# The norm of x for QKV's last four blocks: on GpSimd instead of ScalarE, with loads, stores, moments, turns and parts at other steps

## The reference, cut to what matters

```python
def _layernorm(x, axis=-1, eps=1e-05):
    m = jnp.mean(x, axis=axis, keepdims=True)
    v = jnp.var(x, axis=axis, keepdims=True)
    return (x - m) / jnp.sqrt(v + eps)

# x: (2, 2048, 1024); attention with d = 256, one head
qkv = jnp.einsum('bsc,cf->bsf', _layernorm(x), Wqkv) + bqkv
q, k, v = split(qkv)
x = x + softmax(q @ k.T / 16) @ v @ Wo + bo
# FFN: relu(x @ up)^2 @ down, plus a routed low rank part, and a last layer norm
x = x + _L0_ffn_ref(_layernorm(x), ...)
```

## Time and profile before

| | us |
|---|---|
| median of three runs | 2342.77 (2338.67 to 2347.44) |
| the profiled execution's own time | 2346.55 |
| its span in the trace | 2344.7 |
| PE busy | 2306.0 (98% of the span) |
| VectorE, ScalarE, GpSimd busy | 1584.1, 825.3, 343.5 |
| mean granted TensorE clock | 0.993 of full |
| DMA, whole execution | 581.19 MB, mean 248 GB/s |

### The profile page before, as it was taken

How to read it: one execution, slowest core, us unless ns; L and a number is a source line. 1 busy time by engine, 2 the same in 40 slices (tenths; PEclk the granted TensorE clock), 3 DMA queues, 4 the chain that set the end, 5 groups by cost and what they waited for, 6 DMA issues and landing times.

```text
span 2344.7 us, 27515 instructions
## 1 busy us (share of the span) xinstructions
PE 2306.0 (98%) x10760; PEld 1934.2 (82%) x10760; DVE 1584.1 (68%) x1788; ACT 825.3 (35%) x949; POOL 343.5 (15%) x686
## 2 busy tenths in 40 slices
PE   9989899999999999999999999999999999999998
PEld 8878788888888888888888888888888888888886
DVE  6867658887898956498764368875238876434548
ACT  4335555666555533431212232213132121223211
POOL 2134500000131300032210013310003221000000
PEclk9999999999999999999999999999999999999999
DMA  9899874542233699978997678898668899666875
GB/s 295 291 363 301 305 247 138 209 142 82 96 116 114 232 302 334 329 260 304 346 325 215 190 251 295 324 331 279 190 223 270 306 326 337 208 194 201 244 206 194
DMA packets 242322, 581.19 MB, mean 248 GB/s; under 512 B 27345, under 2 KB 91793, under 8 KB 241937
## 3 DMA queue, kind: packets, MB, share of 16 engines
q1 hardware_dynamic: 160272, 443.56, 58.7%
q10 hardware_dynamic: 81280, 135.55, 15.8%
q0 software_dynamic: 640, 0.33, 0.1%
HBM read 422.25 MB, written 152.90 MB: 245 GB/s over the span
## 4 chain that ended last, share of the span: by engine, by line
PE 83%; DVE 6%; DMA 5%; ACT 2%; POOL 1%; issue 1%; SPq 1%; ACTq 0%; DVEq 0%; POOLq 0%
PE psum L1146 11%; PE psum L1147 11%; PE psum L1148 11%; PE psum L1125 10%; PE psum L1127 10%; PE psum L1126 10%; PE psum L1028 2%; PE psum L1029 2%; PE psum L1030 2%; PE psum L998 2%; PE psum L999 2%; PE psum L1000 2%; DMA RAW<-in_x_dram 1%; PE psum L1088 1%; PE psum L1081 1%
## 5 line engine op out<-in xcount | busy, mean ns | idle before, releaser
L1814 DVE TENSOR_TENSOR HB<-HB,psum 128x1024 f32<-128x1024 f32 x135 | 163.1, 1218 | 298.4 <-PE psum L1127 298.4
L2036 POOL TENSOR_SCALAR veA<-mvA 128x1 f32<-128x1 f32 x32 | 31.3, 977 | 1253.7 <-DVE mvA L1722 1253.7
L1381 ACT ACTIVATE HB<-HB 128x1024 f32<-128x1024 f32 x64 | 67.8, 1060 | 306.9 <-DVE HB L1814 306.9
L1125 PE MATMUL psum<-XS2h,WR 128*128 128x512 f32 x280 | 109.4, 391 | 1.0 <-DVE XS2l L1497 0.6
L1125 PE MATMUL psum<-XS1h,WR 128*128 128x512 f32 x280 | 109.1, 390 | 0.0
L1125 PE MATMUL psum<-XS0h,WR 128*128 128x512 f32 x280 | 109.1, 390 | 0.0
L1125 PE MATMUL psum<-XS3h,WR 128*128 128x512 f32 x280 | 109.1, 390 | 0.0
L1127 PE MATMUL psum<-XS1h,WR 128*128 128x512 f32 x280 | 109.0, 389 | 0.0
L1126 PE MATMUL psum<-XS2l,WR 128*128 128x512 f32 x280 | 109.0, 389 | 0.0
L1127 PE MATMUL psum<-XS2h,WR 128*128 128x512 f32 x280 | 109.0, 389 | 0.0
L1127 PE MATMUL psum<-XS0h,WR 128*128 128x512 f32 x280 | 109.0, 389 | 0.0
(11 more groups left out here) (439 smaller groups left out, 6706.7 us busy)
## 6 DMA issues: line engine op xcount, KB each, us to landing
WR<-wu_s SPq DMA_DIRECT2D x280, 512.0 KB, 4.4
WR<-wd_s SPq DMA_DIRECT2D x280, 512.0 KB, 4.9
att_s<-ATT ACTq DMA_DIRECT2D x32, 516.0 KB, 3.6
RAW<-in_x_dram SPq DMA_DIRECT2D x32, 512.0 KB, 9.4
RES<-x1b_s SPq DMA_DIRECT2D x128, 128.0 KB, 6.0
out_dram<-ZR ACTq DMA_DIRECT2D x118, 128.0 KB, 5.6
xT_s<-XT SPq DMA_DIRECT2D x24, 512.0 KB, 7.5
HB<-xT_s SPq DMA_DIRECT2D x12, 1024.0 KB, 8.8
```

What stands on the lines that cost most here:

```text
L1125: e.matmul(o, w[:, 0, ws], h[:, :, ws], start=kt == 0, stop=False)
L1814: e.tensor_tensor(to, a, src, op=ALU.add).then_inc(*vevac.next(key))
```

## The change

It takes `x_norm` off ScalarE's program. GpSimd does the same 16 operations (tensor_scalar, 128x256, x times RX plus NBX, in place) inside `x_merge`, right behind NBX and ahead of the copies of the moments. `x_turn` waits for GpSimd's signal. Beside it, steps stand at other places:

- the PE turns of x2 at g = 15, 16, 18, 19 (before 13 to 16), those of x3 at 25, 26, 28, 29 (before 25, 27, 29, 31);
- the loads of x5, x6, x7 one or two steps earlier and ahead of what else stands there (`front`), so on SP's queue they come ahead of the loads of quads u5, u7 and u9, where they stood behind these;
- the moments of x4 to x7 in two steps of two, at other steps;
- the turns of x4 to x7 four or five steps later, in the block ahead of their use, and the parts in pairs right behind, up to the first steps of the V tiles (for x4: in the last V tile and in the block's own first step);
- the last store of each of the quads u0 to u9 and d0 one step later.

```diff
-        at(g0, quad, q, [g0 + g for g in ((3, 4, 5, 5, 6, 7) if g0 < 37 else (4, 5, 6, 6, 7, 8))])
+        at(g0, quad, q, [g0 + g for g in ((3, 4, 5, 5, 6, 8) if g0 < 37 else (4, 5, 6, 6, 7, 9))])
...
-    for u, load, moments, norm, turns in ((2, 4, (9, 9, 9, 9), (11, 11, 12, 12), (13, 14, 15, 16)),
-                                          (3, 13, (17, 17, 18, 18), (20, 20, 21, 21), (25, 27, 29, 31))):
+    for u, load, moments, norm, turns in ((2, 4, (9, 9, 9, 9), (11, 11, 12, 12), (15, 16, 18, 19)),
+                                          (3, 13, (17, 17, 18, 18), (20, 20, 21, 21), (25, 26, 28, 29))):
...
     for u in range(4, 8):
-        b = 12 * (u - 1)
-        load, moments, norm, parts = (22, 26, 39, 43) if u == 4 else (b - 17, b - 13, b + 1, b + 5)
+        load, moments, norm = {4: (22, 28, 40), 5: (30, 37, 49), 6: (42, 47, 61), 7: (53, 59, 73)}[u]
         for tt in range(4):
-            at(load, "load_x", u, tt)
-            at(moments + tt, "x_stats", u, tt)
-        at(moments + 3, "x_merge", u)
+            front(load, "load_x", u, tt)
+            at(moments + tt // 2, "x_stats", u, tt)
+        at(moments + 1, "x_merge", u)
         for j in range(4):
-            front(norm + j // 2, "x_norm", u, j)
-            at(norm + 1 + j // 2, "x_turn", u, j)
-            front(parts + j, "x_parts", u, j)
+            at(norm + 5 + j // 2, "x_turn", u, j)
+            front(norm + 7 + j // 2, "x_parts", u, j)
...
-        def x_norm(u, j):
-            on.wait_ge(*inv["x", u])
-            for g in range(4 * j, 4 * j + 4):
-                k = e.activation(x_rows(u)[:, g], x_rows(u)[:, g], AF.Identity, bias=NBX[:, g:g + 1], scale=RX[:, g:g + 1])
-            k.then_inc(*hi.next(("norm", u, j)))
...
         def x_turn(u, j):
             on.wait_ge(*v_mm[u - 2, 3])
-            on.wait_ge(*hi["norm", u, j])
+            on.wait_ge(*inv["norm", u, j])
...
             on.wait_ge(*const["pw"])
-            if u > 4:
-                on.wait_ge(*hi["norm", u - 1, 3])
...
-            e.tensor_scalar(NBX[:, :], NBX[:, :], -1.0, None, op0=ALU.mult, op1=ALU.bypass).then_inc(*inv.next(("x", u)))
+            e.tensor_scalar(NBX[:, :], NBX[:, :], -1.0, None, op0=ALU.mult, op1=ALU.bypass).then_inc(*inv.next())
+            on.wait_ge(*inv.now())
+            for g in range(16):
+                e.tensor_scalar(x_rows(u)[:, g], x_rows(u)[:, g], RX[:, g:g + 1], NBX[:, g:g + 1], op0=ALU.mult,
+                                op1=ALU.add).then_inc(*inv.next(*((("norm", u, g // 4),) if g % 4 == 3 else ())))
```

More of the change, by code:

```diff
@@ L1481, in scalar @@
         do = {"e_split": e_split, "f_split": f_split, "wq_split": wq_split, "wv_split": wv_split, "e2_out": e2_out,
-              "xt_hi": xt_hi, "x_norm": x_norm, "x_parts": x_parts, "qk_out": qk_out, "qk_store": qk_store, "v_store": v_store, "kv_split": kv_split,
+              "xt_hi": xt_hi, "x_parts": x_parts, "qk_out": qk_out, "qk_store": qk_store, "v_store": v_store, "kv_split": kv_split,
               "q_split_a": q_split_a, "q_split": q_split, "S_out": S_out, "m_bc": m_bc, "P_exp": P_exp, "P_h": P_h,
```

## The result

The changed kernel takes 2360.45 us (median of 4 runs, 2356.91 to 2362.61), the kernel before 2340.86 (4 runs): 1.008 of it, 95% interval 1.0067 to 1.0093. It is slower by some 19 us; the prediction said 2338.4, and its range ended at 2356. The profiled execution took 2359.03 us, its span is 2357.2.

A forecast was written before the change was run, and what follows sets the result against it. PE, busy 98% of the span, was taken as the bound, with 39.0 us of losses to win. Gains 7.2 - 4.8 + 1.4 + 0.6 = 4.4 us, from the median 2342.77 to 2338.4; range 2321 to 2356.

The forecast's parts named there:

- 4.8 us worse: Blocks 3 and 4 together: a loss of 21.7 us where the two blocks lose 16.9 in the kernel before.
- nothing else holds OUT; the block ends at 177.7: Block 3: starts at 144.4, ScalarE no longer holds norm or early stores, so it runs without loss.
- the 14.8 us for the loads: Ahead of blocks 4 and 5: time from last turn until x6 and u7, or x7 and u9, have landed.
- 2342.1: Whole kernel: forecast for the profiled execution, 2346.55 less the gain of 4.4 us.
- losses of 39.0 us: QKV stage, blocks 1 to 6: PE's waits and slow stretches, all there is to win, 1.7% of the time.
- 7.2 said: Blocks 1 and 2: gain of 7.2 us, leaving 1.7 of the 8.9 lost.
- The stand at block 4: Start of block 4: PE idles 18.6 us, until 196.3, for loads 14.8, sums 2.6 and a low part 1.2.
- The 3.3: Block 5: PE's wait for the first OUT, ready at 246 to 247 and wanted at 243.7.
- the loads are slower under the quads' stores: Rival, blocks 4 and 5: loads take 21 us, not 14.8, adding 6.3 in block 4; 2345 to 2350, chance 0.16.
- 29.9 + 12 = 42 us: GpSimd's time per block with the norm at 12 us, against PE's 33.4; close, but hidden.
- The first rival: GpSimd becomes the bound as VectorE's turns wait for its norms: slower, up to 2404; chance 0.17.

The follow-up runs named there:

- second profile: The kernel before, unchanged, run and profiled once more: median 2339.66 us, 0.9995 of before; the profiled span is 2337.6 us.
- behind: Changed kernel with the loads of x6 and x7 behind those of quads u7 and u9 again: 2353.16 us, 1.0051 of the kernel before.
- early_act: Kernel before with the changed turns of x2 and x3, moments of x4 and x5 at 28 and 37, quads' last stores one step later: 2334.96 us, 0.9975.
- early_oldstores: early_act with the last stores of the quads at their old steps: 2339.78 us, 0.9993 of the kernel before.
- normonly: Kernel before with only the norm moved to GpSimd, all steps as before: 2344.66 us, 1.0019 of the kernel before.
- early_gp: early_act with the whole norm on GpSimd behind the moments: 2339.39 us, 0.9996 of the kernel before.
- behind_m48_t4: behind with x6's moments one step later (48) and the turns of x4 two steps earlier: 2350.92 us, 1.0040 of the kernel before.
- halfnorm_t4: behind_m48_t4 with 8 of GpSimd's 16 norm instructions left out for each of x4 to x7 (rows go on unnormed): 2340.65 us, 0.9998 of before.
- nonorm_t4: behind_m48_t4 with GpSimd's norm of x4 to x7 left out but for four 8-column operations (blocks unnormed): 2339.20 us, 0.9996 of before.

## Why the prediction was wrong

The prediction put blocks 3 and 4 at 4.8 us worse than in the first profile of before; they are some 15.5 worse (99.2 against 83.7). The steps that failed are "nothing else holds OUT; the block ends at 177.7" (5.3 us) and the 14.8 us for the loads ahead of the stand and again in block 5, which were 17.5 and 19.6. Then comes the base from which the gain was subtracted. Between the executions themselves the miss is 2359.03 - 2342.1 = 16.9 us, about what the stage shows; the rest of the 22 us between 2338.4 and 2360.45 is how far the two executions lay from the medians, 3.8 above and 1.4 below.

**The base.** I summed losses of 39.0 us from one execution. The second profile reaches block 7 at 308.77 instead of 315.22, so there was some 6.5 us less to win: 8.4 and 5.5 less in blocks 3 and 5, 1.6 to 3.4 more in the others. I noted that the execution lay 3.8 above the median and then subtracted the whole gain from the median: that was the fault, and worth at least these 3.8.

**Blocks 1 and 2: right, but the loss was overstated.** 6.3 us were gained, 7.2 said. In all 15 runs with the new turns block 1 took 37.9 us, where the sum has 33.38 + 4 x 0.79 = 36.5 for a block with turn groups and no waits. So 1.4 us of what was counted as lost in that block were not to be had by this change, and the 39.0 was too high by that as well.

**Block 3: "nothing else holds OUT; the block ends at 177.7": wrong by 5.3 us.** PE stood 3.23 at STG, and the clock was 0.96. Rows from VectorE's, ScalarE's and PE's timelines of the changed kernel, with the DMA view's row of u5's load:

```profile
QR1a<-in_upfc_dram SPq DMA_DIRECT2D x1, 1024.0 KB, 11.0
...
152.39 0.69 DVE L1663 TENSOR_TENSOR QR1a<-QR1a 128x512 f32<-128x512 f32 x1 [5.07 <-DMA QR1a<-in_upfc_dram]
...
155.07 0.63 ACT L1314 ACTIVATE QH1a<-QR1a 128x512 fp32r<-128x512 f32 x1 [12.58 <-DVE QR1a L1670]
...
159.05 0.69 ACT L1216 ACTIVATE STG<-psum,bqs 128x512 f32<-128x512 f32 x1 [0.51 <-ACT QH1a L1170]
...
159.79 0.80 PE L956 MATMUL psum<-XA1h,WQH 128*128 128x512 f32 x1 [3.23 <-ACT STG L1216]
```

The same in the first profile of before:

```profile
QR1a<-in_upfc_dram SPq DMA_DIRECT2D x1, 1024.0 KB, 6.2
...
149.22 0.68 DVE L1671 TENSOR_TENSOR QR1a<-QR1a 128x512 f32<-128x512 f32 x1
...
149.60 5.69 ACTq L1234 DMA_DIRECT2D v_s<-OUT  x2
155.34 0.64 ACT L1322 ACTIVATE QH1a<-QR1a 128x512 fp32r<-128x512 f32 x1 [11.57 <-issue]
```

u5's high parts, which stand ahead of the first OUT, start at 155.07 now and at 155.34 before: PE came 6 us earlier, they did not. The two times agree by two different causes. Before, u5 had landed in 6.2 us and its sums were done by 151.83, but ScalarE was still issuing two stores of V, which took it 5.69 us. In the changed kernel u5 is issued at about the same time (141.33, before 140.44) but behind x5, which now stands ahead of it, and takes 11.0 us to land; VectorE stands 5.07 for it. The run behind, which keeps x5 ahead, has 11.2, early_act and early_oldstores, with x5 behind, 5.7 and 5.9. The order that made the stand at block 4 is at work here too, at u5. It is not the only thing that holds: in early_act ScalarE issues stores until 153.99, and PE still waits 2.70. In all runs with the whole early part this wait is 2.7 to 4.1 us. Why these stores take so long to issue is not shown; DMA was busy for 97% of blocks 1 and 2 in the changed kernel.

**The stand at block 4: mechanism right, size wrong**, 24.25 against 18.6. Of the difference 2.6 is the last turn, behind VectorE's wait of 3.55 for u6's high parts; 2.7 the loads, 17.5 against 14.8, more even than the 16.9 that the prediction had for u7 wholly behind x6; 0.4 sums and parts. The chain was as written, and the run behind shows that SP's order makes 18 of the 24 us.

**Block 5: mechanism right.** The last turn of x5 ended 28.0 us after block 4's start, as said (28.1). The loads took 19.6, not 14.8, sums and high parts 7.0 (256.00 to 263.02), not 6.1, and OUT began another 1.1 later, since ScalarE issued a store of V first. The wait at OUT was 9.10, not 3.3, with no second one:

```profile
264.89 0.80 PE L956 MATMUL psum<-XA1h,WQH 128*128 128x512 f32 x1 [9.10 <-ACT OUT L1216]
```

The 3.3 was itself at the high end of its sum: 224.4 + 14.8 + 2.6 + 3.5 and one OUT of 0.7 make 246.0, 2.3 behind 243.7. The rival "the loads are slower under the quads' stores" had 21 us for the loads: nearer in block 5, not in block 4, where 17.5 lies nearer to 14.8, though its stand of 18.6 + 6.3 = 24.9 came near by making up for the late turn. Its 2345 to 2350 lacked block 3 and the base.

**GpSimd: the price about right, the verdict half.** The norms took 12.44, 18.54, 10.40 and 12.46 us, 13.5 on the mean, against 12. In the changed kernel x5's norm ended at 224.33 and its first turn began at 224.79, just hidden. But my cycle of 29.9 + 12 = 42 us was 44.5 to 46.3, and I looked only at turns waiting for it, not at STX, which the moments of the next block need. Against the norm on ScalarE in the same schedule, the whole norm on GpSimd cost 4.4 (normonly), 4.4 (early_gp) and 5.9 us (behind_m48_t4). In the changed kernel itself no wait of VectorE for GpSimd reaches 1 us up to block 7, and no run takes the norm off GpSimd there: that it is a second cause of its loss is not shown, only that it would be the next one once the loads are in order. The first rival named the right engine and the wrong wait.

**Block 7.** I took nothing; PE waited 1.67 at OUT.

What stays open: why x6 in the run behind, with u7 landed before it is issued, and the last part of x7 in halfnorm_t4 and nonorm_t4 take more than 17 us to come. The 9 us that nonorm_t4 still loses at OUT in block 5 follow from this by the chain of block 3 before (moments, the quad's last low part, its last store, OUT), as read from its trace; no run tests it.

## What to carry to other kernels

Before a load is put ahead of another on a queue, ask what each of them waits for: the one whose buffer comes free last belongs behind, or all behind it waits too. Before work is moved to an engine that looks 15% busy, work out its cycle per block with all waits for DMA in it and compare with the block's time, and look for every buffer that this engine frees, not only for its result. And take the losses that a change may win from more than one profile: here two executions of one program differed by 7 us in just the waits that the change was meant for.

## What was not expected of the hardware

GpSimd's 128x256 tensor_scalar takes as long as VectorE lets it. Two norms of 16 instructions, from GpSimd's timeline in early_gp and then in the changed kernel:

```profile
245.88 8.60 POOL L2117 TENSOR_SCALAR RAW<-RAW,RX,NBX 128x256 f32<-128x256 f32 x16
```

```profile
205.79 18.54 POOL L2116 TENSOR_SCALAR RAW<-RAW,RX,NBX 128x256 f32<-128x256 f32 x16
```

In the first, VectorE ran no operation with two SBUF inputs, in the second 13.4 us of them (sums, high-low differences of quads, low parts). Between these lie 2.3 us of them with 10.8, 5.7 with 12.4, 8.0 with 14.6, 10.3 with 16.0: 8.6 us and some 0.7 us for each microsecond of such work. A line through all 36 such norms of nine runs has 8.4 and 0.72. VectorE's busy share alone doesn't order them: 6.0 of 8.6 us in the first, 7.3 of 10.8 in another of early_gp's. The Trainium skill (SBUF — State Buffer, SBUF: two separate sides) says that a VectorE operation with two SBUF inputs and a GpSimd operation that reads SBUF exclude each other for the whole instruction. By an estimate from that each microsecond would cost one, and the runs show 0.7. Part of the gap may be that VectorE's rows hold waits of their own: its 128x512 operations in the second norm took 0.68 to 0.93 us; this is not shown. Undisturbed, an instruction of the norm takes 0.54 us; the estimate from the Trainium skill (GPSIMD Engine Reference, Performance versus the Vector engine) was 0.4. For 16 that makes 6 us, where the prediction has 7; nothing rested on it.
